# The step sizes' polynomial, norm's shift and the lag of the second matmuls in a Mamba and mixture-of-experts kernel

## The reference

```
xc, z = silu(conv(x @ in_proj)), second half of x @ in_proj
dt = softplus(x_dbl[:, :1] @ dt_w + dt_b)               # the step sizes
dA = min(exp(dt * A), 1);  dBu = dt * B * xc
states: a scan over the tokens in chunks of 32, y = sum over states of state * C
out = (y + xc * D) * silu(z) @ out_proj
```

## Time and profile before

| | |
|---|---|
| median of 3 runs | 1546.16 us (1543.6 to 1546.69) |
| the profiled execution | 1545.74 us, its span 1544.0 us |
| busy in the span | PE 1303.9, DVE 1232.6, ACT 1052.9, POOL 666.0 us |
| granted TensorE clock, mean | 0.922 of 2.4 GHz |
| first scan instruction, last one starts | 50.8 us, 566.7 us |

### The profile page before, as it was taken

The page is one execution under the profiler, slowest core; times in us unless marked ns, Lnnn a source line. Parts: engine busy times, 40 slices in busy tenths (PEclk is TensorE's granted clock), DMA queues, the critical chain, the costliest instruction groups (busy, mean ns, idle before and its releaser), DMA issues.

```text
span 1544.0 us, 22558 instructions
## 1 busy us (share of the span) xinstructions
PE 1303.9 (84%) x8408; PEld 504.2 (33%) x8408; DVE 1232.6 (80%) x1471; ACT 1052.9 (68%) x1831; POOL 666.0 (43%) x625
## 2 busy tenths in 40 slices
PE   4364679889975997887589999999999998999998
PEld 1111234333342443332212222222222222235963
DVE  0899998998999783676689999999999998933522
ACT  3542378758845744643269998999899987997653
POOL 0688868976986775662403113111211123111430
PEclk9676799989987998998679999999999998999999
DMA  8122223322321412312213101100010000010210
GB/s 221 64 82 68 74 72 89 82 70 84 92 65 50 101 40 55 72 43 37 34 54 50 30 29 48 23 2 2 2 23 2 2 2 18 6 29 10 75 31 28
DMA packets 63696, 75.71 MB, mean 49 GB/s; under 512 B 8633, under 2 KB 39226, under 8 KB 63458
## 3 DMA queue, kind: packets, MB, share of 16 engines
q1 hardware_dynamic: 62818, 72.70, 18.0%
q0 software_dynamic: 768, 1.57, 0.3%
HBM read 66.04 MB, written 8.21 MB: 48 GB/s over the span
## 4 chain that ended last, share of the span: by engine, by line
PE 47%; DVE 29%; issue 9%; POOL 8%; ACT 5%; DMA 1%; SPq 1%; another core or an unknown queue 0%; DVEq 0%; POOLq 0%; ACTq 0%
DVE mx L1652 15%; PE PS L962 12%; PE PS L950 6%; PE PS L919 4%; PE PS L738 4%; PE PS L729 4%; DVE D L1443 4%; POOL D L1895 2%; PE PS L1034 2%; PE PS L1049 2%; DVE PS L1429 2%; DVE PS L1435 2%; PE PS L1070 2%; PE PS L1058 2%; PE PS L685 2%
## 5 line engine op out<-in xcount | busy, mean ns | idle before, releaser
L1319 ACT ACTIVATE aa<-PS 128x512 f32<-128x512 f32 x1024 | 551.6, 597 | 64.6 <-PE PS L950 53.2
L1652 DVE TENSOR_REDUCE mx<-PS 128x2 f32<-128x1024 f32 x480 | 553.1, 1216 | 16.8 <-PE PS L919 10.6
L962 PE MATMUL PS<-aa,D 128*32 128x256 f32 x4096 | 324.3, 394 | 1.6 <-ACT aa L1319 0.6
L950 PE MATMUL PS<-D 54*128 54x512 bf16 x1024 | 214.0, 393 | 12.9 <-ACT aa L1319 8.3
L919 PE MATMUL PS<-D 51*128 51x512 bf16 x960 | 191.7, 387 | 17.2 <-DVE mx L1652 16.2
L2009 POOL CAST n<-nm 4x512 bf16<-4x512 f32 x15 | 9.1, 604 | 455.0 <-ACT nm L1301 455.0
L1429 DVE TENSOR_TENSOR_SCAN PS<-PS,D 128x512 f32<-128x512 f32 x128 | 157.5, 1230 | 11.2 <-POOL D L1911 3.5
L738 PE MATMUL PS<-xnT,f_w 128*128 128x512 f32 x288 | 157.6, 640 | 5.6 <-ACT HB L1209 5.3
L1209 ACT ACTIVATE HB<-PS 128x512 f32<-128x512 f32 x144 | 85.0, 596 | 111.3 <-PE PS L738 103.3
L729 PE MATMUL PS<-HB,f_w 128*128 128x512 f32 x288 | 144.5, 612 | 3.9 <-DVE GO L1522 3.6
L962 PEld LDWEIGHTS PS<-aa,D 128*32 128x32 f32 x4096 | 84.4, 109 | 193.8 <-issue 155.3
(11 more groups left out here) (327 smaller groups left out, 1713.1 us busy)
## 6 DMA issues: line engine op xcount, KB each, us to landing
D<-bc SPq DMA_DIRECT2D x128, 256.0 KB, 3.6
GB<-gd SPq DMA_DIRECT2D x32, 256.0 KB, 4.2
D<-sc SPq DMA_DIRECT2D x72, 64.0 KB
aa<-in_L_ffn_W SPq DMA_DIRECT2D x9, 256.0 KB, 3.2
D<-in_L_ffn_W SPq DMA_DIRECT2D x9, 256.0 KB, 3.6
f_w<-in_L_ffn_experts_w SPq DMA_DIRECT2D x1, 2048.0 KB, 9.2
f_w<-in_L_ffn_experts_w SPq DMA_DIRECT2D x8, 256.0 KB, 6.1
aa<-gh SPq DMA_DIRECT2D x1, 2048.0 KB, 9.0
```

The lines of the kernel that those rows point to most:

```text
L950: e.matmul(take_exp(s + hh), KS[64 * hh:64 * hh + 54, p, 128 * kb:128 * kb + 128], QP[64 * hh:64 * hh + 54, qc % 2, p, :], start=True, sto ...
L962: t = e.matmul(PS[32 * j:32 * j + 32, 7, cs], va[:, kb, 9 * h:9 * h + 32], Pt[K % 3][:, 512 * j + 256 * n:512 * j + 256 * n + 256], start= ...
L1319: e.activation(Pt[K % 3][:, c:c + 512], bank((s + hh) % 3), ACT.Exp).then_inc(S("e_free"), 1)
L1652: e.tensor_reduce(mx4[:, G % 2, b, 2 * pair:2 * pair + 2, c:c + 1], max_banks(m), AX.X, ALU.max).then_inc(freed(m)[0], 1)
```

## The change

It has four parts. The polynomial becomes `LEAD * e *` the product of three quartics ((e + s0)^2 + s1)^2 + more: ScalarE makes two squares in a row, the second of the first's output, VectorE one add-and-multiply, in three rounds. The shift moves to GpSimd's `power`: one operation (-mean) ahead of the power and a multiply behind it; the second layer's norms keep to two. The second matmuls of chunks 0 to 2 go four or five steps behind the first instead of two or three, and with them `gate_expert`, `add` and the rows of gates: (1) from step 10 to 12, (7) from 34 to 36, (8) from 37 to 38, the last four second matmuls together in step 37. The last feed-forward keeps its order. And `prolog`'s `DU` comes earlier, with the step sizes.

```diff
-                for r in range(5):
+                for r in range(3):
                     for g in range(2):
...
+                        e.activation(SQ[g], yy2[g], ACT.Square, bias=cst[:, 2 * r:2 * r + 1]).then_inc(S("s_sq"), 1)
+                        w.wait_ge(S("s_sq"), n + 1)
                         if r:
                             w.wait_ge(S("s_pp"), 2 * r + g - 1)
-                        e.activation(bank(7 - g), yy2[g], ACT.Square, bias=cst[:, r:r + 1]).then_inc(S("s_sq"), 1)
+                        e.activation(bank(7 - g), SQ[g], ACT.Square, bias=cst[:, 2 * r + 1:2 * r + 2]).then_inc(
+                            S("s_sq"), 1)
...
                     if tc < 3 and n <= 8:
-                        for u in {6: (0, 1), 7: (2, 3), 8: (4, 5, 6)}.get(n, ()):
-                            down(36 * tc + u)
...
+                    elif n < 8:
+                        for u in {6: (0, 1), 7: (2, 3)}.get(n, ()):
+                            down(36 * tc + u)
+                    else:
+                        if n % 4 == 1:
+                            down(i - 5)
+                        if n % 4:
+                            down(i - 4)
...
+                    for u in range(32, 36):
+                        down(36 * tc + u)
...
             def norm(i, tc, st, pre, pause=2):
-                yield from idle(pause)
-                w.wait_ge(S(pre + "_pw"), i + 1)
-                e.scalar_tensor_tensor(out=shift[:, st:st + 4], in0=mv[:, st:st + 4, 0], scalar=-1.0,
-                                       in1=rstd[:, st:st + 4], op0=ALU.mult, op1=ALU.mult).then_inc(S(pre + "_shift"), 1)
-                yield from idle(2)
+                yield from idle(pause + 2)
...
             def power(i, st, pre, each=3):
                 e.tensor_scalar(rstd[:, st:st + 4], mv[:, st:st + 4, 1], 1e-5, None, ALU.add).then_inc(
+                    S(pre + "_pw"), 1)
+                if each == 3:
+                    e.tensor_scalar(shift[:, st:st + 4], mv[:, st:st + 4, 0], -1.0, None, ALU.mult).then_inc(
+                        S(pre + "_pw"), 1)
+                w.wait_ge(S(pre + "_pw"), n + each - 1)
                 e.tensor_tensor(rstd[:, st:st + 4], rstd[:, st:st + 4], mhalf[:, 0:4], ALU.pow).then_inc(
                     S(pre + "_pw"), 1)
+                if each == 3:
+                    w.wait_ge(S(pre + "_pw"), n + 3)
+                    e.tensor_tensor(shift[:, st:st + 4], shift[:, st:st + 4], rstd[:, st:st + 4], ALU.mult).then_inc(
+                        S(pre + "_shift"), 1)
```

More of the change, by code:

```diff
@@ L758, in ffn @@
                 yield
-                yield from idle(2)
+                yield from idle(2 if tc == 3 else 1)
             def later(tc):
@@ L1166, in prolog @@
                     w.wait_ge(S("p_dl"), 2 * tc + g)
[L1167 to L1171, removed]
+                    for r in range(3):
+                        n = 6 * i + 2 * r
+                        w.wait_ge(S("p_sq"), n)
+                        e.activation(SQ[r % 2], ey[g], ACT.Square, bias=cst[:, 2 * r:2 * r + 1]).then_inc(S("p_sq"), 1)
+                        w.wait_ge(S("p_sq"), n + 1)
+                        e.activation(SQ[r % 2] if r else bank(7), SQ[r % 2], ACT.Square,
+                                     bias=cst[:, 2 * r + 1:2 * r + 2]).then_inc(S("p_sq"), 1)
                         yield from idle(2)
@@ L1386, in start @@
                 drain(norm(0, 0, 0, "p"))
-                for r, (_, im) in enumerate(PAIRS):
+                for r, (_, _, more) in enumerate(QUARTICS):
                     for g in range(2):
@@ L1390, in start @@
                             w.wait_ge(S("s_pp"), 2 * r + g - 1)
-                        w.wait_ge(S("s_sq"), 2 * r + g + 1)
-                        e.scalar_tensor_tensor(out=pp2[g], in0=bank(7 - g), scalar=im * im, in1=pp2[g] if r else yy2[g],
+                        w.wait_ge(S("s_sq"), 4 * r + 2 * g + 2)
+                        e.scalar_tensor_tensor(out=pp2[g], in0=bank(7 - g), scalar=more, in1=pp2[g] if r else yy2[g],
                                                op0=ALU.add, op1=ALU.mult).then_inc(S("s_pp"), 1)
                 for g in range(2):
-                    w.wait_ge(S("s_pp"), 9 + g)
+                    w.wait_ge(S("s_pp"), 5 + g)
                     w.wait_ge(S("s_vv"), g + 1)
@@ L1525, in ffn @@
             def ffn(tc):
+                later_by = 0 if tc == 3 else 2
                 for n in range(36):
-                    if n % 4 == 2 and n >= 10:
-                        gate_expert(tc, n // 4 - 1)
+                    if n % 4 == (2 + later_by) % 4 and n >= 10 + later_by:
+                        gate_expert(tc, (n - later_by) // 4 - 1)
+                    yield
+                if tc < 3:
+                    gate_expert(tc, 7)
                     yield
@@ L1536, in ffn @@
                 e.tensor_tensor(xs, xs, bank(SUM_BANK[tc]), ALU.add).then_inc(S("x_ffn"), 1)
-                yield
-                yield
+                yield from idle(2 if tc == 3 else 1)
             def later(tc):
@@ L1881, in prolog @@
                 for g in range(2):
-                    yield from idle(12)
+                    yield from idle(8)
                     w.wait_ge(S("p_dl"), 2 * tc + g + 1)
@@ L1923, in add @@
                     e.tensor_tensor(FO[:, :], FO[:, :], GO[x % 2], ALU.add).then_inc(S("ffn_sum"), 1)
+                later_by = 0 if tc == 3 else 2
                 for n in range(36):
-                    if n % 4 == 2 and n >= 10:
-                        add(n // 4 - 1)
+                    if n % 4 == (2 + later_by) % 4 and n >= 10 + later_by:
+                        add((n - later_by) // 4 - 1)
+                    yield
+                if tc < 3:
+                    add(7)
                     yield
@@ L1931, in ffn @@
                 yield
-                yield from idle(3)
+                yield from idle(3 if tc == 3 else 2)
             def later(tc):
@@ L2051, in project @@
             def project(q, m):
-                power(q, 4 * q, "h")
-                w.wait_ge(S("h_pw"), q + 1)
+                power(q, 4 * q, "h", 2)
+                w.wait_ge(S("h_pw"), 2 * q + 2)
                 w.wait_ge(S("h_st"), 8 * q + 8)
```

59 lines of the change are left out of this document (31 added, 28 removed).

## The result

The changed kernel takes 1531.76 us (median of five runs, 1529.25 to 1533.2), the kernel before in the same session 1546.16: a ratio of 0.9913 with a 95% interval of 0.9895 to 0.9932, 13.4 us less. The forecast was 1530 and "faster". Its total held; two of its terms did not, and two of its own signs failed: the last unit is 13.55 us earlier and `gate_expert(8)` behind it 10.3, where some 18 and 16 were due.

A forecast was written before the change was run, and what follows sets the result against it. VectorE's in-order stream bounds the scan, TensorE the third feed-forward behind its gates. Terms -1.2 + 5.4 + 12.0 + 2.5 - 1.7 - 0.6 = 16.4 us gained, 1546.2 to 1530 as a median (chance 0.68), range 1524 to 1534.

The forecast's parts named there:

- two of its own signs: Scan's end: last VectorE instruction some 18 us earlier than 568, gate_expert(8) behind it some 16 earlier than 573.66.
- The shift: Norms: moving it off VectorE gains 12.0 us; GpSimd's longer way loses 0.6 at the path's end, 0.3 in the start.
- The two kinds of place: VectorE's stream: three shifts at 1.0 us (prologs 1, 2, first later), four at 2.5 (three epilogs, second later).
- the reverse hold: Norms: VectorE could hold GpSimd's new two-input multiply; at worst GpSimd loses 5.6 us, under its idle time.
- The start: Up to the first scan at 50.8 us: polynomial 0.9 us later, shift 0.3 us more, 1.2 us lost.
- The rounds: Prologs in the scan: 12 fewer VectorE rounds at 0.45 us each, 5.4 us gained, 1.8 in each of three chunks.
- The squares: ScalarE in the scan: two squares in a row, some 1.4 us a round instead of 0.7, costed at nothing while covered.
- The lag: First two feed-forwards: 2.5 us gained at the first gate_expert, 1.7 lost net at gate_expert(8).
- The third feed-forward: TensorE sets its end: VectorE's gains behind G return as a longer last wait; a 0.9 us bubble is offset.
- its two named terms: Range around 1530: both new waits gone gives 3.4 us more; small operations at the power's price three times, 2.5 less.
- Rival (1): First two feed-forwards: TensorE takes over, 3.6 and 2.5 us return as waits, 10.3 us gained, 1536; chance 0.21.
- Rival (4): Feed-forwards: TensorE's work thins to 1.2 GHz; 16.4 us at low clock eats the gain, 35 give 1565; chance 0.03.

The follow-up runs named there:

- E1: The kernel before with only norm's shift moved from VectorE to GpSimd; ratio 0.9913 to the kernel before.
- E0: The changed kernel again, unaltered, on another chip; ratio 0.9931 to the kernel before.
- E7: The kernel before, shift still on VectorE but as four one-column instructions with a single SBUF tensor input each; ratio 0.9982 to the kernel before.
- after: The changed kernel with all four parts, as traced in one execution of 1531.76 us; ratio 0.9913 to the kernel before.
- E4: The changed kernel with second matmuls catching up from unit 20, so the last ones and the last gate_experts stand as before; ratio 0.9951 to the kernel before.
- E5: The changed kernel with ScalarE's exp of the gates one step earlier; ratio 1.0002 to the kernel before.
- E6: The changed kernel with three unused TensorE products ahead of the last four second matmuls; ratio 0.9955 to the kernel before.
- F1: The changed kernel with one pair of squares of prologs 2 and 3 a step later on ScalarE, behind the gates' exp; ratio 0.9927 to the kernel before.
- F2: E6 plus three unused TensorE products (six in the third feed-forward) ahead of the transposes of G; ratio 0.9942 to the kernel before.
- F3: F2 with the five quadratics of the kernel before in place of the new polynomial; ratio 0.9974 to the kernel before.
- E2: The kernel before with only the polynomial changed, five rounds to three with two squares each; ratio 1.0021 to the kernel before.
- E3: The kernel before with only the later order of second matmuls, gate_expert, add and rows of gates; ratio 1.0034 to the kernel before.
- F4: F1 and F2 together, plus both groups' first squares ahead of the second ones in the start; ratio 0.9939 to the kernel before.

## Why the prediction held, step by step

**The shift: 12.0 gained, 0.6 and 0.3 lost; measured 13.4 alone** (E1, 0.9913 of 1546). The two kinds of place were right: from the first scan to unit 2, in which prolog 1's shift stood, the lead grows by 1.40 us (forecast 1.0), at the first epilog's by 2.68 (2.5). In E0 and E1 the latter is 1.02 and 1.49 us, less by waits of 1.62 and 1.14 us at the residual add, which the forecast did not have. The mechanism was right (E7), and the reverse hold that the prediction weighed did not happen. GpSimd's new operations are short, all twenty of them:

```profile
L1888 POOL TENSOR_TENSOR rstd<-rstd,mhalf 128x4 f32<-128x4 f32 x10 | 10.4, 1038 | 0.8
...
L1885 POOL TENSOR_SCALAR shift<-mv 128x4 f32<-128x4 f32 x10 | 2.3, 228 | 0.8
L1892 POOL TENSOR_TENSOR shift<-shift,rstd 128x4 f32<-128x4 f32 x10 | 2.0, 203 | 0.8
```

A power's 1038 ns did not stand for a multiply; the copy's 210 did.

**The start: 1.2 lost; measured 1.31.** The polynomial's 0.9 is 0.96. The shift's 0.3 was there in `xn` in E1 and after (0.28 and 0.35), in E0 it was 0.07, and it did not reach the scan in E1. Executions with the changed start differ by more: the first scan is 0.70 to 1.80 us later in E0, E4, E5, E6, F1 and F2. So only the 0.96 is shown.

**The rounds: 5.4 gained.** 1.7 us between units 2 and 15, where 1.8 was due. **The squares, "costed at nothing while this cover holds": this step failed**, by its own condition. At the gates' exp the cover is gone, and the wait grows from 0.59 to 1.86 us, twice, which also makes TensorE idle 3.8 us instead of 2.8 ahead of G. Net, the polynomial is worth 4.9 us with shift and lag (F2, F3; by the forecast 5.4 - 0.9 = 4.5), and costs 3.2 alone (E2).

**The lag: 2.5 gained at the first `gate_expert`, 1.7 lost at the last.** Both were mis-sized. At the first the wait fell by 2.56 and 3.82 us in E3, by 0.35 and 1.79 in after. The low clock behind G (0.72) and the squares took the rest: with the clock at 1.00 (F2) the two waits are 1.16 and 1.25 us shorter than in after, and with the old polynomial besides (F3) another 1.05 and 0.78. At the last it is 3.5 us for 1.7; it is 1.87 where TensorE is idle for at most 1.25 us ahead of it (E6, F2, F3, F4). The forecast's 3.7 us for the eight records was their price at 2.4 GHz, and half of them ran at 1.2. Alone the lag costs 5.3 us, where the forecast had 0.8 gained.

**The third feed-forward** was right in kind (the last waits, 4.03 and 3.79, together exceed 5.13) and 0.7 us longer than before. But the lag costs there as well, which the forecast had at nothing ("a bubble of 0.9 us ... is offset"): from G to `gate_expert(8)` it is 1.5 us longer with the lag alone (E3), and 2.0 shorter than in E0 where the last second matmuls stand as before (E4). At unit 55 the lead is 10.97 where 17.0 was due. Of the 6.0 us missing, 3.7 are the doubled waits and some 2.5 the gates' exp, twice. The tail gave 1.6 us back between `gate_expert(8)` and G of the last chunk, and 2.1 behind it, where only two of the twelve shifts stood (0.15 and 0.16 us). That last part can't be told from chance: the stretch from the last G to the end was 930.7 to 940.4 us in the twelve other traces, in order by session and not by kernel.

So the likeliest case came in, with a total 2 us off (1530 against 1531.76), on a shift that gave 2 more and a lag that gave 6 less. That the total came so close is in part luck: at `gate_expert(8)` of the third feed-forward, behind all that the forecast counts but its last 0.6 us, the lead is 10.3 us and not 16, and what lies behind, in which it counted on 0.6 lost, gave 3.7 more. The range of 1524 to 1534 was wider than its two named terms make it (1526.6 to 1532.5 around 1530); the result lies in both. The measured prices of the parts, 13.4 + 4.9 - 5.3 = 13.0, stand beside the 13.4 and 10.7 of the whole. They do not simply add up, though: with the polynomial's price alone (E2, 3.2 lost) the sum is 4.9. Rival (1) is real in E1 and E2, where the lag is missing. Rival (4) had the right engine at the wrong scale: not a whole feed-forward at the low clock, but stretches of a few us, at two places of the first one (0.72 over 6.0 us, 0.61 over 3.6).

Not settled: why E4, F2 and F4, whose traces are near their medians and lead E0's or after's at the last unit, are no faster in time. The third feed-forward accounts for 2.5 us in F2 and F4, and for none in E4. F2's and F4's leads are also against a trace of another session. (E6's and F1's leads are largely those of one execution.) And why the lag with F2's products (F3, 0.9974) is 9 us over the shift alone (E1, 0.9913): their traces differ by 0.3 us at the last unit and by 5.6 at the last G, and the rest, between two sessions, is not placed.

## What to carry to other kernels

A term priced at TensorE's full speed holds only if TensorE has work right up to it. Where an edit makes TensorE wait for one result and then run a short burst that others wait for, price the burst at both levels, and look for the place where a queue has no slack instead of the stage's mean share. Make the parts of a change one by one: here the cheapest part alone gave the whole gain, one part lost alone, and one paid only beside another. And ask of every tiny VectorE instruction with two SBUF inputs what GpSimd does at that moment.

## What the runs showed of the hardware

- TensorE's clock after a short idle stretch differs from one execution to the next. Of ten groups of eight records behind 2.35 to 3.82 us of idle (after, E0, E3, E5, F1), six took 5.2 to 6.3 us and four 3.70; behind at most 1.25 us of idle they took 3.65 to 3.70 in all thirteen (the third feed-forward of after, E0, E3, E5 and F1, and the first two of E6, F2, F3 and F4). The Trainium skill's page "TensorE: Matmul & The Clock Gate", in "Part 1: The HAM clock gate", says that the gate's look at the engine is not aligned with the kernel, so that the low-clock stretches of one kernel vary from run to run. E0 and after, the same program, agree: 3.70 and 5.40 us at the same place.
- A VectorE instruction of 128 x 4 with a single SBUF input can be held too. The gates' normalization, 0.17 us in after, took 1.12 in E5, beside a GpSimd product, and ended 0.03 us behind it. In the kernel before it took 0.46 us (221.71 to 222.17), beside a product that ended at 222.15. The one-column instructions of E7 were not held, so the number of SBUF inputs alone does not decide:

```profile
215.97 2.34 POOL L1922 TENSOR_TENSOR wb<-D 128x1024 f32<-128x1024 f32 x1
...
217.22 1.12 DVE L1518 TENSOR_SCALAR mx<-mx 128x4 f32<-128x4 f32 x1
```
